# Indirect DMAs that wait for the preceding one's instruction instead of for a clear of a dead tile

## The reference

```python
edge_index = jnp.stack([src, dst])
x = _layernorm(x + _L0_gnn_ref(x, edge_weight, edge_attr_3, edge_index, ...))   # messages from x[src], summed by dst
x = _layernorm(x + _L1_gnn_ref(x, edge_index))       # three hops: x = segment_sum(norm * x[src], dst)
x = _layernorm(x + _L2_gnn_ref(x, edge_index, edge_attr_32, ...))   # MLP on x[src], x[dst]; segment_max by dst
x = _layernorm(x + _L3_gnn_ref(x, edge_attr3_2x32, src, dst, ...))  # attention softmax by dst, then a sum by dst
return x
```

## Time and profile before

| | us |
|---|---|
| median of 3 runs | 1860.24 |
| lowest, highest | 1854.67, 1861.78 |
| span of the profiled execution | 1863.2 |
| GpSimd busy in it | 1400.9 |
| VectorE busy in it | 1344.3 |
| TensorE busy in it | 729.3 |
| ScalarE busy in it | 488.0 |

### The profile page before, as it was taken

One profiled execution on the slowest core, in us unless ns is written; L12 is line 12 of the kernel. 1 busy time (PEld: TensorE's weight loads), 2 busy tenths in 40 slices (PEclk: granted clock), 3 DMA queues, 4 the chain that ended last, 5 costly groups with the idle time before them and its releaser, 6 DMA issues.

```text
span 1863.2 us, 14783 instructions
## 1 busy us (share of the span) xinstructions
PE 729.3 (39%) x3676; PEld 546.2 (29%) x3676; DVE 1344.3 (72%) x2600; ACT 488.0 (26%) x1014; POOL 1400.9 (75%) x2019
## 2 busy tenths in 40 slices
PE   7912555541450003605337001456605656551400
PEld 3301222220220003605326001355505655551400
DVE  9955999986999645775755882478785999986400
ACT  7822311110110013522334200233302343342100
POOL 8878887888888885868878558884068888888776
PEclk9966778775785556867678555677757776665655
DMA  8165511111111101412222330000001111110000
GB/s 321 38 211 194 184 32 32 32 26 17 26 20 50 42 20 59 137 65 76 99 88 102 140 137 4 5 23 13 30 20 24 32 28 26 32 29 9 10 10 10
DMA packets 64097, 114.29 MB, mean 61 GB/s; under 512 B 27599, under 2 KB 48648, under 8 KB 63224
## 3 DMA queue, kind: packets, MB, share of 16 engines
q1 hardware_dynamic: 24304, 80.96, 12.0%
q0 software_dynamic: 33728, 12.79, 4.9%
q10 hardware_dynamic: 5960, 19.43, 2.8%
HBM read 61.66 MB, written 55.21 MB: 63 GB/s over the span
## 4 chain that ended last, share of the span: by engine, by line
POOL 75%; issue 17%; DVE 5%; PE 1%; DMA 1%; ACT 0%; POOLq 0%; SPq 0%; DVEq 0%
POOL A_dst L746 12%; POOL A_src L746 12%; POOL out L880 12%; POOL gtmp L736 9%; POOL work L746 8%; POOL A_msg L746 7%; POOL A_msg L823 7%; POOL edge_sums L829 5%; POOL out_short L746 3%; DVE A_dst L1484 1%; DVE stat L1495 1%; DVE work L2276 0%; DVE A_sum L1484 0%; PE bank L1388 0%; DVE A_dst L1492 0%
## 5 line engine op out<-in xcount | busy, mean ns | idle before, releaser
L746 POOL DMA_INDIRECT A_dst<-in_x,dst_i x196 | 224.3, 1144 | 57.4 <-POOL gtmp L736 39.1
L736 POOL MEMSET gtmp<- 64x64 f32 x934 | 156.5, 168 | 144.6 <-DMA table<-A_dst 110.9
L880 POOL DMA_INDIRECT out<-A_dst,out_i x196 | 217.9, 1112 | 59.7 <-POOL gtmp L736 34.3
L1495 DVE TENSOR_REDUCE work<-work 128x80 f32<-128x1280 f32 (+3 forms) x147 | 204.6, 1421 | 78.8 <-issue 50.2
L1310 PE MATMUL bank<-w2fold,work 128*128 128x384 f32 x392 | 183.1, 611 | 173.0 <-DVE work L1484 162.7
L746 POOL DMA_INDIRECT A_src<-x_pos,A_tmp x140 | 147.2, 1051 | 40.5 <-POOL gtmp L736 24.4
L746 POOL DMA_INDIRECT work<-table,pos_i x112 | 144.9, 1294 | 31.1 <-POOL gtmp L736 23.5
L1235 PE MATMUL bank<-ident,work 128*128 128x128 f32 (+1 forms) x294 | 63.4, 327 | 264.1 <-ACTq L995 139.2
L1310 PEld LDWEIGHTS bank<-w2fold,work 128*128 128x128 f32 x392 | 86.0, 237 | 269.5 <-issue 227.1
L746 POOL DMA_INDIRECT A_msg<-table,pos_i x112 | 139.0, 1241 | 32.4 <-POOL gtmp L736 16.5
L1484 DVE TENSOR_TENSOR work<-bank,work 128x384 f32<-128x384 f32 (+1 forms) x294 | 153.6, 590 | 0.2
(11 more groups left out here) (396 smaller groups left out, 2335.5 us busy)
## 6 DMA issues: line engine op xcount, KB each, us to landing
work<-in_x SPq DMA_DIRECT2D x26, 960.0 KB
x_pos<-A_sum SPq DMA_DIRECT2D x13, 990.0 KB
out<-work ACTq DMA_DIRECT2D x13, 960.0 KB
A_tmp<-ew_turned_rows ACTq DMA_DIRECT2D x49, 130.0 KB
table<-A_dst SPq DMA_DIRECT2D x2, 3136.0 KB
edge_sums<-A_dst SPq DMA_DIRECT2D x2, 3136.0 KB
table<-A_dst SPq DMA_DIRECT2D x13, 448.0 KB
A_tmp<-in_edge_attr_2x SPq DMA_DIRECT2D x49, 112.0 KB
```

The source lines that it names most:

```text
L736: pool.memset(tile, 0.0).then_inc(cleared, 1)
L746: pool.indirect_dma_start(out=column(t), out_offset=None, in_=of, in_offset=bass.IndirectOffsetOnAxis(ap=idx[:, t:t + 1], axis=0), bounds_ ...
L880: pool.indirect_dma_start(out=out, out_offset=bass.IndirectOffsetOnAxis(ap=out_i[:, t:t + 1], axis=0), in_=A_dst[:, t, :], in_offset=None, ...
L1495: return v.tensor_reduce(out=o, in_=a, axis=AX, op=op)
```

## The change

A new semaphore `move_issued` takes the place of `cleared`. Each indirect DMA carries it as `engine_sem`: it is raised by one when GpSimd has finished its instruction, beside the semaphore that the landing data raise as before. `follow` replaces `pause` and issues nothing; it makes the next DMA wait until `move_issued` has reached the number of DMAs before it. The clears go. The wait also comes to the DMAs that had no clear: the 84 gathers of step 1 and the last 36 scatters. Only the DMAs inside conditional branches, for lists longer than the data here have, stay without it.

```diff
-            def pause(tile):
-
-                issued["cleared"] += 1
-                pool.memset(tile, 0.0).then_inc(cleared, 1)
-                pool.wait_ge(cleared, issued["cleared"])
-
-            def gather(column, of, idx, limit, done, columns=range(T), keep=None, cleared_tile=None):
+            def follow():
+
+                if issued["moves"]:
+                    pool.wait_ge(move_issued, issued["moves"])
+                issued["moves"] += 1
+
+            def gather(column, of, idx, limit, done, columns=range(T), keep=None, spaced=True):
 
                 for t in columns:
                     if keep:
                         keep()
-                    if cleared_tile is not None:
-                        pause(cleared_tile)
+                    if spaced:
+                        follow()
                     pool.indirect_dma_start(
                         out=column(t), out_offset=None, in_=of,
                         in_offset=bass.IndirectOffsetOnAxis(ap=idx[:, t:t + 1], axis=0),
-                        bounds_check=limit, oob_is_err=False).then_inc(done(t), 16)
+                        bounds_check=limit, oob_is_err=False,
+                        engine_sem=move_issued if spaced else None).then_inc(done(t), 16)
...
                     if keep and keep(t):
                         pool.wait_ge(n_out, keep(t))
-                    pause(gtmp[0:HF])
-                    move(t).then_inc(done, 16)
+                    follow()
+                    move(t, spaced=True).then_inc(done, 16)
...
                 for t in range(T)[c] if isinstance(c, slice) else range(c * GATHER_CHUNK, (c + 1) * GATHER_CHUNK):
-                    if i < 6:
-                        pause(gtmp[0:HF])
+                    follow()
                     pool.indirect_dma_start(
                         out=out, out_offset=bass.IndirectOffsetOnAxis(ap=out_i[:, t:t + 1], axis=0),
                         in_=A_dst[:, t, :], in_offset=None, bounds_check=node_limit,
-                        oob_is_err=False).then_inc(scattered, 16)
+                        oob_is_err=False, engine_sem=move_issued).then_inc(scattered, 16)
```

More of the change, by code:

```diff
@@ L261, in gnn_kernel @@
         short_ready = sem("short_ready")
+        move_issued = sem("move_issued")
         few_done, more_done, rest_done = sem("few_done"), sem("more_done"), sem("rest_done")
@@ L773, in _ @@
             pool.wait_ge(pos_stored, 32)
-            gather(lambda t: pos_x[:, t:t + 1], pos_table, src_i, node_limit, lambda t: pos_rows, range(plain),
-                   cleared_tile=gtmp[0:HF])
+            gather(lambda t: pos_x[:, t:t + 1], pos_table, src_i, node_limit, lambda t: pos_rows, range(plain))
             for k in range(XP_SLOTS):
@@ L779, in _ @@
             gather(lambda t: src_wide[:, t, :], x_pos, src_i, node_limit, lambda t: src_rows[t // GATHER_CHUNK],
-                   range(plain, T), cleared_tile=gtmp[0:HF])
-            gather_dst(range(DST_FIRST * GATHER_CHUNK, T), None, gtmp[0:HF])
+                   range(plain, T))
+            gather_dst(range(DST_FIRST * GATHER_CHUNK, T), None)
             pool.wait_ge(short_ready, 1)
@@ L813, in second_columns @@
                 for t in range(FEWEST2):
-                    pause(gtmp[0:HF])
-                    move(t).then_inc(hop_done, 16)
+                    follow()
+                    move(t, spaced=True).then_inc(hop_done, 16)
                 with pool.If(n2 > FEWEST2):
@@ L822, in take_short @@
             def take_short(column, of, idx):
-                return lambda t: pool.indirect_dma_start(
+                return lambda t, spaced=False: pool.indirect_dma_start(
                     out=column(t), out_offset=None, in_=of,
                     in_offset=bass.IndirectOffsetOnAxis(ap=idx[:, t:t + 1], axis=0),
-                    bounds_check=edge_limit, oob_is_err=False)
+                    bounds_check=edge_limit, oob_is_err=False,
+                    engine_sem=move_issued if spaced else None)
             def put_short(of, idx, column):
-                return lambda t: pool.indirect_dma_start(
+                return lambda t, spaced=False: pool.indirect_dma_start(
                     out=of, out_offset=bass.IndirectOffsetOnAxis(ap=idx[:, t:t + 1], axis=0),
-                    in_=column(t), in_offset=None, bounds_check=edge_limit, oob_is_err=False)
+                    in_=column(t), in_offset=None, bounds_check=edge_limit, oob_is_err=False,
+                    engine_sem=move_issued if spaced else None)
             pool.wait_ge(table_stored, 16 * parts_until(0))
@@ L864, in _ @@
                         gather(lambda t: of[:, t, :], tables[k], pos_i, edge_limit, lambda t: wide_rows,
-                               range(c * GATHER_CHUNK + SLOTS_IN_WINDOW, (c + 1) * GATHER_CHUNK))
+                               range(c * GATHER_CHUNK + SLOTS_IN_WINDOW, (c + 1) * GATHER_CHUNK), spaced=False)
                     pool.wait_ge(wide_rows, 16 * CHUNKS * (GATHER_CHUNK - SLOTS_IN_WINDOW) * (k - 2))
@@ L872, in _ @@
                     gather(lambda t: of[:, t, :], tables[k], pos_i, edge_limit, lambda t: here,
-                           range(c * GATHER_CHUNK, c * GATHER_CHUNK + SLOTS_IN_WINDOW), cleared_tile=gtmp[0:HF])
+                           range(c * GATHER_CHUNK, c * GATHER_CHUNK + SLOTS_IN_WINDOW))
             for i, c in enumerate(LAST_ORDER):
```

7 lines of the change are left out of this document (3 added, 4 removed).

## The result

The changed kernel takes 2182.7 us (median of 4 runs, 2171.88 to 2190.01) against 1857.65 us (4 runs, 1854.67 to 1861.78): a ratio of 1.174, 95% interval 1.170 to 1.178. It is slower by 17% where 6% less was forecast. The profiled execution took 2171.88 us, its span is 2170.1 us, 307 us over the span before.

What follows compares the result with a forecast made beforehand. GpSimd's row of 1054 indirect DMAs was taken as the bound. Savings of 51 + 16 + 15.7 + 37 = 120 us, less 5, gave a 1748 us span and 1745 us forecast (0.64); range 1705 to 1820 us.

Steps and rivals of the forecast that it cites:

- Nothing changes on other engines' queues: Whole kernel: each added wait stands on GpSimd's queue, so only the next DMA is behind it; no cost elsewhere.
- the first stage: 136 to 720 us, 364 paused position and row gathers: 51 us saved, all counting against VectorE's 65.5 us of waits.
- GpSimd's own terms: Indirect DMAs: distance 1.30 us instead of 1.44, gap 0.30, saving 0.14 per paused DMA; scatters at the end stay 1.29.
- 15.7 forecast: 1088 to 1281 us, first pass of 112 window gathers: 15.7 us saved, all of it counting.
- GpSimd's busy time: Whole span: falls by about the clears' 156.5 us to 1245 to 1260 us.
- The 10 us for stalls of denser work: DMAs beside VectorE's denser work: 10 us more stalls, half given back for fewer gaps, so 5 us off the saving.
- VectorE's waits: Waits for gathers fall from 65.5 to about 14 us between 136 and 720 us, from 16 to nearly none until 1060.
- Rival A: Wait on preceding DMA: semaphore comes late, 0.07 us on top of the 0.30 us gap; about 1805 us, chance 0.17.
- Rival D: Every DMA: semaphore rises only when data have landed, 2.4 us on top of 1.3; near 4000 us, chance 0.02.
- Rival C: More than forecast: clears gone also free VectorE from the shared port pair; 1717 or about 1705 us, chance 0.05.
- Rival B: Stretches with VectorE busy: without clears DMAs lengthen to 1.35 us, distance 1.65; slower, 1892 us, chance 0.12.
- wrong if: Mean DMA length moves over 0.05 us, or stage shifts differ from 51, 67, 83, 120 us at 720, 1060, 1281, 1863.

Runs made afterwards that it cites:

- The kernel with a distance of 1.37 us: The changed kernel, its chain of waits and posts kept, plus one unwaited 64x64 clear in front of each DMA: 1937.92 us.

## Why the prediction was wrong

**What failed** is one sentence of it: "Nothing changes on other engines' queues", and with it the rule by which every stage was summed, that a saving on GpSimd counts until its consumer is late. The consumers' pace was taken from the trace of before as if it were their own. It was not. Units of TensorE, ScalarE and VectorE ran at two in 5.8 us while GpSimd's DMAs were 1.44 us apart, and at 1.30 us they ran at one in 11.2 us. The failing term is in the first stage, -51 us forecast and +207 measured. After the first hop another 100 us were lost: 50 up to the window gathers and 110 in the fourth layer, where the same late posts stand, less 62 that GpSimd made good.

**GpSimd's own terms were right, up to the length of a DMA.** The gap of 0.30 us, the distance of 1.30 us, 1.29 us at the end, the 56 gathers beside the histogram (73.3 us busy in both) came as said. So 0.14 us per DMA was saved: GpSimd was through with the gathers of the radial stretch 59 us sooner, and needed 168 us (1345.9 to 1513.8) for the window gathers that had taken 193, 25 us less against 15.7 forecast. The second pass of window gathers took 155 us in place of 189, 34 us less.

**GpSimd's busy time** fell to 1173 us, further than the 1245 to 1260 us forecast: 71 us beyond the clears, 0.07 us per DMA and so outside the 0.05 us that the prediction allowed itself. The 10 us for stalls of denser work had the wrong sign. That VectorE's work is spread over 307 us more may be part of the reason, but not all: with the 64x1 clear VectorE's work lies closer than before, and the mean DMA is shorter all the same (1.132 us, against 1.174 before and 1.105 changed).

**VectorE's waits.** Those for gathers did go between 136 us and the first hop, and gave way to waits with no owner, after (us in total, times, longest):

```profile
DVE work L1485 <- remote: 194.8, 27, 9.6
DVE work L1485 <- issue: 86.6, 12, 9.6
```

281 us of them where 65.5 us had been waited for gathers.

**Rival A** (the semaphore comes late, 1805 us) is refuted by the 0.30 us gap. The prediction had set a rule against the change: the recorded end is the last descriptor written, while the cores finish later (the Trainium skill, "Perfetto Trace Analysis", section "DMA Instruction — SWDGE (GPSIMD)"). What the prediction drew from it, a semaphore that trails the recorded end, doesn't show here: a DMA with the wait and one without start after the same 0.30 us. **Rival D** (it rises at landing) is refuted by the same row. **Rival C** (1705 us) didn't come; GpSimd alone gained more than forecast, 9 us in the first pass of window gathers and some 18 in the second, and the total had nothing of it.

**Rival B** said "it is not the wait but the clear that keeps DMAs short", slower, 1892 us. It had the right suspect and the wrong victim. The clear matters, by the distance that it makes, but a DMA without it is as short as ever (1.00 us); what the distance kept short was the time from the end of TensorE's instructions to the start of those who wait for them. And it was priced at 32 us for want of any row that showed such an effect. The rows could have raised the doubt. The unpaused gathers beside the histogram are 1.66 us apart, on the safe side of the edge. DMAs 1.30 us apart stood in the trace of before in two places only the earlier trace rows, before 136 us and at the end, and TensorE had little or nothing to do there: 34 matmuls between 93 and 136 us, none from 1810 us on. The saving was carried over to a stretch with 283 matmuls in 300 us, a state that no row showed.

**What the words "wrong if" caught.** The prediction named the shifts at four points. The first of them, +207 us in place of -51 at the first hop, shows at once where to look. GpSimd's own rows don't: by themselves they look like a success.

## What to carry to other kernels

A small instruction that does nothing may be pacing its engine for the sake of others; before it is removed, ask which distances it sets, and try it smaller before trying it gone. Here the clear cut from 64x64 to 64x1 keeps the distance at 1.38 us and gains 2.3%, while no clear at all costs 17 to 24%, in executions that are all recorded by the profiler. When waits grow that the profile puts down to "remote", "issue" or an unknown queue on one core, take the difference between the end of the posting instruction and the start of the waiting one, unit by unit along the span, and look at who starts and stops being busy where it jumps. When the profile of one kernel lacks records that the profile of the other has, count them first: a time taken with the recording on may then be a time of the recording.

## What the runs showed of the hardware

- **In these recorded executions TensorE's instructions are known late beside dense GpSimd DMAs.** With indirect DMAs 1.30 us apart, one recorded matmul or weight load gets through per 1.40 us (11.20 us for 8, 16.80 us for 12, 56.00 us for 40), with the added semaphore, with its wait, or with neither; VectorE's and ScalarE's posts took 0.03 to 0.15 us at the same time. The lateness is the queue of what is under way: 17.8 us with two units, 29.0 with three, 44.5 with three units of twelve instructions each.
- **The edge is narrow.** The kernel with a distance of 1.37 us loses 72 us and the one with 1.38 us gains 41; they differ in the chain as well. Backlog takes some 10 to 40 us of dense DMAs to appear and some 25 us to drain once they stop.
- The Trainium skill, "VectorE: DVE Perf Modes", section "The TRN2 errata — SBUF-src ops pay a fixed extra latency per instruction", warns that semaphore adds at a high rate from one engine can deadlock another, and that kernels with dense adds on completion from several engines should space them. Spacing is what helped here, but no run locked up, and it was GpSimd's DMAs that had to be spaced: taking their added posts away didn't help, and the delay went with TensorE's instructions rather than its posts. Whether it is the same weakness no run here shows.
- **A semaphore add and a wait for it by GpSimd cost nothing between two DMAs**: 1.30 us with none and with one pair. Six pairs left most gaps at 0.30 us and made 12 of 205 longer than 1 us.
- **A clear's cost depends on where it stands**: 64x64 takes 0.17 us in the radial stretch and 0.80 us beside the histogram, where VectorE and TensorE are busy all the time (77.0 of 77 us each in the kernel before). 64x32 took 0.14 us on average, 64x1 still 0.12.
- **The profile loses records where GpSimd's DMAs are dense**: 16.6 rises of a semaphore per DMA at a mean distance of 1.51 us, 2.4 at 1.34 us.
- What lies between GpSimd and TensorE is open, and whether it is the recording itself: the runs show a rate and a backlog, not a part of the chip. For the 50 us lost in the hops and the node pass behind them the posts were not followed.
